# Two of a group's four value products issued one and two steps behind the turning of the maxima, instead of in front of it and in the next group

## The chip, the cores and the metric

One core of a Trainium2 chip runs the kernel. The metric is device time in microseconds (us). The kernel before took 1863.36 us (median of 3 runs, 1863.1 to 1865.16). A profiled execution of it took 1858.42 us.

## The reference

Four sequences of 512 tokens with 256 features go through four blocks: a cross-attention with 16 heads of 64, a gated fusion, a causal attention with 16 heads of 16, and a decoder layer with a banded self-attention (window 64), a full cross-attention (both 16 heads of 16) and a feed-forward part. The change touches the three attentions with heads of 16 only. Each computes, per head:

```python
s = jnp.einsum('bhqd,bhkd->bhqk', q, k) / jnp.sqrt(DH)
s = s + bias[None]                       # banded only
s = jnp.where(mask, s, -1e9)             # causal and banded
a = jax.nn.softmax(s, axis=-1)
o = jnp.einsum('bhqk,bhkd->bhqd', a, v)
```

## The kernel before, in words

The four sequences (B = 4) run one after the other in a hardware loop. In each, the three attentions with small heads follow each other: a = CAUSAL, BANDED, FULL. An attention's 16 heads are worked in GROUPS = 4 groups g of four heads, and the 512 rows in NT = 4 tiles of 128.

A group needs the scores twice. **Step A**(g, qt, u) (`pass_a`, L1220) is a pair of TensorE products, two heads u, queries in rows. VectorE takes their row maxima (`maxima`, L906). When the eight A of a group are through, **step M** (`maxima_cols`) splits the maxima into two bf16 halves. **Step T** (`turn_maxima`, L1267) turns them on TensorE, and ScalarE copies the turned rows into the query tile (`maxima_rows`, L675, two copies a group), so that the second pass of scores comes out with the maximum subtracted. **Step B**(g, kt, u) (`pass_b`, L1237) is that second pass with keys in rows; ScalarE exponentiates it (`exponentials`, L683). **Step V**(g, kt) (`values`, L1256) multiplies four heads' exponentials of key tile kt with the values and adds into a bank of `obank`; it waits for the exponentials of both B of its tile. **Step H**(g) (`head_out`) divides by the row sums on VectorE once V(g, 3) is done. Causal and banded products get masks added by further small products (L1206). Widths: 512 for every FULL product; 512, 384, 256, 128 for the causal B and V of kt 0 to 3 (A the other way round); 192 or 128 for banded ones. After the last group `out_heads` (L1296) projects; in the banded attention one projection stands before it.

A, B and T write to `ring`, which has SLOTS = 3 places. Each takes the place of the A, B or T three before it in the order of `group_steps`, and waits (`start`) until that one has been evacuated: A by VectorE, B and T by ScalarE. V writes to `obank` and takes no place in the ring. TensorE works in the order of `group_steps`; VectorE takes A, M and H from the same list, ScalarE B and T. Nothing overtakes on an engine. Groups overlap: while group g does its B and V, the A of group g+1 (second half) and of g+2 (first half) run between them.

The order of a middle group before, written as "B20" for B(g, 2, 0), A by its number 0 to 7 in its group, and V by kt:

```
i=0  B00  A4(g+1)  V2(g-1)
i=1  B01  A5(g+1)  V3(g-1)
i=2  B10  A6(g+1)
i=3  B11  A7(g+1)  M(g+1)  H(g-1)
i=4  B20  V0  T(g+1)  A0(g+2)  V1
i=5  B21  A1(g+2)
i=6  B30  A2(g+2)
i=7  B31  A3(g+2)
```

In group 2 the second half has no A, in group 3 there is none at all and no T; group 3 ends with V2, V3, H.

Of the kernel before, what the change touches and what calls it, by code (L numbers as in the profile page):

```python
# [29 lines left out]
NT = S // P  # L30
DT = D // P
H = 16
# [51 lines left out]
def ahead(g, n):  # L84

    return [("A", g) + divmod(n, 2)] if g < GROUPS else []


def group_steps(g):

    steps = []
    if g == 0:
        steps += ahead(1, 0) + ahead(1, 1) + [("T", 0)] + ahead(1, 2) + ahead(1, 3)
    for i in range(2 * NT):
        steps.append(("B", g) + divmod(i, 2))
        if i < NT:
            steps += ahead(g + 1, NT + i)
            if i < 2 and g:
                steps.append(("V", g - 1, 2 + i))
            if i == NT - 1:  # L100
                steps += [("M", g + 1)] if g + 1 < GROUPS else []
                steps += [("H", g - 1)] if g else []
            continue
        if i == NT:
            steps.append(("V", g, 0))
            steps += [("T", g + 1)] if g + 1 < GROUPS else []
        steps += ahead(g + 2, i - NT)
        if i == NT:
            steps.append(("V", g, 1))
    if g == GROUPS - 1:  # L110
        steps += [("V", g, 2), ("V", g, 3), ("H", g)]
    return steps


def attention_jobs(a):
    jobs = [(a, "A", 0, qt, u) for qt in range(NT) for u in range(2)]
    for g in range(GROUPS):
        jobs += [(a,) + step for step in group_steps(g) if step[0] in "ABT"]
    return jobs
# [33 lines left out]
def build(nc, io, out):  # L153
    with ExitStack() as ctx:
# [407 lines left out]
        def _(act):  # L562
# [20 lines left out]
            with act.Fori(0, B) as b:  # L583
# [102 lines left out]
                def attention(a):  # L686
                    for g in range(GROUPS):
                        for kind, *which in group_steps(g):
                            if kind == "T":
                                maxima_rows(a, *which)  # L690
                            if kind == "B":
                                if which == [0, NT - 1, 0]:
                                    for k in range(1, GROUPS):
                                        act.wait_ge(k_stacked[k], (b * 3 + a + 1) * 96)
                                exponentials(a, *which)
# [26 lines left out]
        def _(dve):  # L722
# [10 lines left out]
            with dve.Fori(0, B) as b:  # L733
# [201 lines left out]
                def attention(a):  # L935
                    for qt in range(NT):
                        for u in range(2):
                            maxima(a, 0, qt, u)
                    maxima_cols(a, 0)
                    for g in range(GROUPS):  # L940
                        for kind, *which in group_steps(g):
                            if kind == "A":
                                maxima(a, *which)
                            if kind == "M":
                                maxima_cols(a, *which)
                            if kind == "H":
                                head_out(a, *which)
# [501 lines left out]
```

How the kernel before makes its waits and increments, by code:

```python
        @block.sync  # L361
# [30 lines left out]
            def stack(a, b):  # L392
                k_high, k_low, q_high, q_low = ((0, 0), (3, 0)), ((1, 1),), ((0, 0), (1, 0)), ((3, 1),)
                sp.wait_ge(*drained_by(K_JOB[a], b))
                if a == CAUSAL:
                    sp.wait_ge(tiles_reset, b * TILES_RESET + TILES_RESET)
                else:
                    sp.wait_ge(*filled_by((a - 1, "B", GROUPS - 1, NT - 1, 1), b))
                    sp.wait_ge(q_preset, b * 2 * GROUPS + a * GROUPS)
                if a != BANDED:
                    sp.wait_ge(k_split, b * 3 + a + 1)
                    for g in range(GROUPS):
                        stack_k(a, b, g, k_high + k_low)
                    sp.wait_ge(q_hi_ready, (b * 3 + a + 1) * DT)
                    stack_q(a, b, 0, q_high)
                else:
                    stack_k(a, b, 0, k_high)
                    sp.wait_ge(q_hi_ready, (b * 3 + a + 1) * DT)
                    stack_q(a, b, 0, q_high)
                    sp.wait_ge(k_split, b * 3 + a + 1)
                    stack_k(a, b, 0, k_low)
                sp.wait_ge(*drained_by(Q_JOB[a], b))
                stack_q(a, b, 0, q_low)
                for g in range(1, GROUPS):
                    if a == BANDED:
                        stack_k(a, b, g, k_high + k_low)
                    stack_q(a, b, g, q_high + q_low)
# [16 lines left out]
                for t in range(NT):
                    sp.wait_ge(*filled_by(("V0", t), b))
                if b:
```

## Time and profile before

| | |
|---|---|
| median of 3 runs | 1863.36 us (1863.1 to 1865.16) |
| profiled execution | 1858.42 us, span 1856.3 us |
| granted TensorE clock, mean over the span | 0.948 of 2.4 GHz |
| busy: TensorE products, VectorE, ScalarE, GpSimd | 87%, 51%, 40%, 14% of the span |

A timeline row gives the start and the length in us, the engine (PE is TensorE, DVE VectorE, ACT ScalarE), the line, the operation, what it writes and reads, how many were merged, and in brackets how long the engine had been idle and who ended that. Products overlap, so the length of one is longer than the time until the next starts. The busy share is a mean over stages with different limits.

### The profile page before, as it was taken

Reading aid. Unit: us, or ns where it says so; the run is one execution under the profiler, and the core shown is the slowest. Engines: PE = TensorE matmul, PEld = TensorE weight load, DVE = VectorE, ACT = ScalarE, POOL = GpSimd, SP = SyncE. Lnnn points to the kernel's source line nnn. Section 1 sums busy time; section 2 is a strip of 40 time slices with the busy share of each in tenths; the row PEclk is TensorE's granted clock in tenths of the full one; section 3 lists DMA queues with packets and bytes.
Section 4 is the critical chain, followed back from the end, with each engine's and each line's share of the span. In section 5 each row is a group of like instructions: output and inputs, shape, how many; then the busy total and the mean of one; then the engine's idle time right before and its main releaser. Section 6 shows DMA issues by size and latency. Waiting matters only on the chain.

```text
span 1856.3 us, 27261 instructions
## 1 busy us (share of the span) xinstructions
PE 1623.5 (87%) x9592; PEld 816.9 (44%) x9592; DVE 949.5 (51%) x2240; ACT 737.9 (40%) x1281; POOL 254.0 (14%) x116
## 2 busy tenths in 40 slices
PE   5999898788999988888999898887899989888786
PEld 2226545434423655532532455553353255455234
DVE  2662655482465365547165447445616535645651
ACT  1652343254263233417236225252624621614352
POOL 1012111201101302110110221111011031112102
PEclk9999999899999899989999889898999998999899
DMA  8001103402100110340210021133111003022300
GB/s 320 1 6 35 35 2 69 94 10 108 47 1 6 35 35 15 56 102 1 108 47 1 7 44 25 33 70 70 42 69 45 1 8 60 9 52 51 59 23 12
DMA packets 44868, 84.17 MB, mean 45 GB/s; under 512 B 10416, under 2 KB 28592, under 8 KB 44464
## 3 DMA queue, kind: packets, MB, share of 16 engines
q1 hardware_dynamic: 44288, 78.42, 17.9%
q10 hardware_dynamic: 432, 3.83, 0.5%
q8 instruction: 86, 1.41, 0.3%
q14 instruction: 62, 0.51, 0.1%
HBM read 42.37 MB, written 2.10 MB: 24 GB/s over the span
## 4 chain that ended last, share of the span: by engine, by line
issue 35%; PE 33%; DVE 17%; ACT 7%; POOL 4%; SPq 3%; DMA 1%; DVEq 0%; ACTq 0%; POOLq 0%
PE ring L1045 6%; PE ring L1024 5%; DVE nmax L906 4%; DVE region_d L790 3%; PE obank L1017 3%; PE ring L1296 2%; PE obank L1256 2%; ACT region_e L607 2%; PE ring L1220 2%; SPq L382 2%; PE ring L1036 2%; ACT region_e L683 2%; PE ring L1237 2%; POOL q_all L530 2%; PE ring L1055 1%
## 5 line engine op out<-in xcount | busy, mean ns | idle before, releaser
L906 DVE TENSOR_REDUCE nmax<-ring 128x2 f32<-128x1024 f32 (+4 forms) x384 | 318.6, 854 | 179.4 <-PE ring L1206 116.7
L683 ACT ACTIVATE region_e<-ring 128x1024 f32<-128x1024 f32 (+4 forms) x384 | 268.9, 733 | 117.7 <-PE ring L1206 73.3
L790 DVE CUSTOM_DVE_ANT_0 region_d<-ring,maskb 128x512 f32<-128x512 f32 x256 | 165.8, 686 | 118.0 <-issue 117.8
L607 ACT ACTIVATE region_e<-region_d,nmin 128x512 f32<-128x512 f32 x256 | 182.6, 714 | 92.1 <-DVE nmin L790 86.1
L675 ACT ACTIVATE q_all<-ring 2x1024 fp32r<-2x1024 bf16 x96 | 97.6, 1016 | 256.1 <-PE ring L1267 255.6
L1017 PE MATMUL obank<-cbf 128*128 128x512 bf16 x672 | 174.1, 402 | 0.0
L1206 PE MATMUL ring<-cbf 64*128 64x128 bf16 (+1 forms) x2048 | 159.2, 240 | 0.0
L1083 PE MATMUL obank<-region_e,vs 128*64 128x512 f32 x512 | 139.9, 630 | 15.1 <-DVE vs L776 15.1
L1073 PE MATMUL ring<-region_q 64*128 64x512 f32 x512 | 141.3, 636 | 5.4 <-ACT region_q L596 5.4
L1220 PE MATMUL ring<-k_tiles_a,q_all 64*128 64x512 f32 (+4 forms) x384 | 84.2, 447 | 62.9 <-DMA q_all<-q_parts 51.7
L541 POOL TENSOR_TENSOR nat_x<-nat_n,rows 128x1024 f32<-128x1024 f32 x16 | 39.1, 2446 | 605.9 <-DVE nat_n L871 605.9
L1220 PE MATMUL ring<-k_tiles_b,q_all 64*128 64x512 f32 (+4 forms) x384 | 79.5, 410 | 23.3 <-ACT q_all L675 12.7
L1017 PEld LDWEIGHTS obank<-cbf 128*128 128x128 bf16 x672 | 63.4, 101 | 81.0 <-issue 24.1
L1237 PE MATMUL ring<-q_all,k_tiles_a 64*128 64x512 f32 (+4 forms) x384 | 79.7, 410 | 14.2 <-DVE nmax L906 11.8
L1237 PE MATMUL ring<-q_all,k_tiles_b 64*128 64x512 f32 (+4 forms) x384 | 74.6, 408 | 13.2 <-ACT q_all L675 8.5
L1220 PEld LDWEIGHTS ring<-k_tiles_a,q_all 64*128 64x128 f32 x384 | 41.1, 210 | 102.1 <-DMA q_all<-q_parts 48.5
L1296 PE MATMUL ring<-w_out,region_d 128*128 128x256 f32 x384 | 85.7, 381 | 0.0
L1073 PEld LDWEIGHTS ring<-region_q 64*128 64x128 f32 x512 | 39.7, 185 | 103.7 <-issue 93.2
L978 DVE TENSOR_TENSOR nat_y<-ring,nat_x 128x512 f32<-128x512 f32 x16 | 11.1, 692 | 138.9 <-PE ring L1045 123.3
L1256 PE MATMUL obank<-region_e,region_b 128*32 128x192 f32 (+4 forms) x1024 | 80.4, 390 | 1.4 <-ACT region_e L683 0.8
L515 POOL TENSOR_TENSOR q_all<-zero 128x2048 fp32r<-128x2048 f32 x8 | 28.8, 3623 | 382.9 <-PE ring L1073 382.9
L1055 PE MATMUL ring<-wvo,ctx_t 128*128 128x512 f32 x128 | 58.1, 609 | 25.3 <-ACT kcol L578 19.2
(169 smaller groups left out, 2291.4 us busy)
## 6 DMA issues: line engine op xcount, KB each, us to landing
q_all<-q_parts SPq DMA_DIRECT2D x288, 64.0 KB, 2.3
k_tiles_a<-k_parts SPq DMA_DIRECT2D x144, 64.0 KB, 2.3
k_tiles_b<-k_parts SPq DMA_DIRECT2D x144, 64.0 KB, 2.3
region_b<-in_w_f SPq DMA_DIRECT2D x8, 1024.0 KB, 5.1
wvo<-in_wv SPq DMA_DIRECT2D x4, 1024.0 KB, 8.9
wqk<-in_wq SPq DMA_DIRECT2D x4, 1024.0 KB, 11.1
wqk<-in_wk SPq DMA_DIRECT2D x4, 1024.0 KB, 13.1
wvo<-in_wo SPq DMA_DIRECT2D x4, 1024.0 KB, 5.6
```

What stands on the lines that cost most here:

```text
L607: ins = act.activation(e0[:, n % E0, h, :], sm0[:, n % 2, h, :], ACT.Exp, bias=nmin0[:, n, h:h + 1], scale=-1.0, accum_out=sum0[:, n, h:h ...
L683: act.activation(e16[:, n % 4, 2 * u:2 * u + 2, 0:nq], slot((a, "B", g, kt, u))[:, :, 0:nq], ACT.Exp)\
L790: ins = dve.tensor_tensor_reduce(out=sm0[:, n % 2, h, :], in0=slot(("S0", p, kt))[:, h, :], in1=maskb[:, :], scale=-1.0, scalar=3.0e38, op ...
L906: dve.tensor_reduce(nmax[:, qt, 2 * u:2 * u + 2], slot(name)[:, :, 0:nk], AX.X, ALU.max, negate=True)\
L1017: pe.matmul(obank[:, 0, :], cb("ident", P), cb("keyrows", S), start=True, stop=True)
L1073: ins = pe.matmul(dst[:, h, :], qk0[own, p % 2, 1, kt * P:(kt + 1) * P], qk0[own, p % 2, 0, :], start=True, stop=True)
L1083: ins = pe.matmul(obank[DK0 * h:DK0 * (h + 1), p % 2, :], vs0[:, n % 4, h, :], e0[:, n % E0, h, :], start=(kt == 0), stop=(kt == NT - 1))
L1206: ins = pe.matmul(dst[:, i, lo:lo + n], cb("halves", P, own, at=half * P), cb(table, n, own, at=half * whole + at), start=False, stop=(hal ...
L1220: ins = pe.matmul(dst[:, i, 0:nk], q_tiles[g][own, u, qt * P:(qt + 1) * P], k_tiles[g][own, u, k0:k0 + nk], start=True, stop=(a == FULL))
L1237: ins = pe.matmul(dst[:, i, 0:nq], k_tiles[g][own, u, kt * P:(kt + 1) * P], q_tiles[g][own, u, q0:q0 + nq], start=True, stop=(a == FULL))
L1256: ins = pe.matmul(obank[32 * s:32 * s + 32, (PAIRS + o) % 2, q0:q0 + nq], v_of[a][:, kt, h, :], e16[:, n % 4, s, 0:nq], start=(kt == 0), s ...
L1296: ins = pe.matmul(dst[j][:, i, 0:D], oT[:, t, m * P:(m + 1) * P], w_out[a][:, t, :], start=(t == 0), stop=(t == GROUPS - 1))
```

## The change

The second value product of a group is issued one step behind the T step (behind A1 of the group after next), and the third one step later (behind A2) instead of at the next group's first step. The fourth stays where it was. In the last group V1 and V2 follow B21 and B30, and only V3 is left behind B31. No instruction is added or dropped.

```diff
@@ group_steps
         if i < NT:
             steps += ahead(g + 1, NT + i)
-            if i < 2 and g:
-                steps.append(("V", g - 1, 2 + i))
+            if i == 1 and g:
+                steps.append(("V", g - 1, NT - 1))
@@
             steps.append(("V", g, 0))
             steps += [("T", g + 1)] if g + 1 < GROUPS else []
         steps += ahead(g + 2, i - NT)
-        if i == NT:
-            steps.append(("V", g, 1))
+        if NT < i < 2 * NT - 1:
+            steps.append(("V", g, i - NT))
     if g == GROUPS - 1:
-        steps += [("V", g, 2), ("V", g, 3), ("H", g)]
+        steps += [("V", g, NT - 1), ("H", g)]
```

The order of a middle group after:

```
i=0  B00  A4(g+1)
i=1  B01  A5(g+1)  V3(g-1)
i=2  B10  A6(g+1)
i=3  B11  A7(g+1)  M(g+1)  H(g-1)
i=4  B20  V0  T(g+1)  A0(g+2)
i=5  B21  A1(g+2)  V1
i=6  B30  A2(g+2)  V2
i=7  B31  A3(g+2)
```

## Rows read from the trace of the kernel before

**Rows 1.** Windows view, first sequence: causal, banded, full attention; busy us by engine, PEclk
```profile
core 0: us, PE busy (x) PEld busy (x) DVE busy (x) ACT busy (x) POOL busy (x), PEclk, DMA share, GB/s
206.59:256.59 50.00, 44.89 (x560) 23.88 (x559) 34.60 (x58) 29.82 (x40) 6.76 (x4) 1.00 0.09 16
288.86:334.35 45.49, 39.36 (x559) 25.97 (x559) 25.40 (x55) 22.23 (x40) 6.69 (x4) 0.93 0.30 53
364.33:431.77 67.44, 56.57 (x319) 18.72 (x319) 46.62 (x55) 39.50 (x40) 0.00 (x0) 0.91 0.13 26
```
**Rows 2.** Lines view by form: maxima, exponentials at full width, copies of the turned maxima
```profile
L906 DVE TENSOR_REDUCE nmax<-ring 128x2 f32<-128x1024 f32 x160 | 189.2, 1220 | 65.1 <-PE ring L1220 61.4 <-PE ring L1206 3.5
...
L683 ACT ACTIVATE region_e<-ring 128x1024 f32<-128x1024 f32 x160 | 157.8, 1028 | 53.0 <-PE ring L1237 36.9 <-PE ring L1206 14.3
...
L675 ACT ACTIVATE q_all<-ring 2x1024 fp32r<-2x1024 bf16 x96 | 97.6, 1016 | 256.1 <-PE ring L1267 255.6
```
**Rows 3.** Timeline, causal attention, from one T step to the next
```profile
222.83 0.62 PE L1267 MATMUL ring<-cbf,mcol 128*128 128x128 bf16 x8
...
223.49 2.04 ACT L675 ACTIVATE q_all<-ring 2x1024 fp32r<-2x1024 bf16 x2 [1.15 <-PE ring L1267]
...
223.76 0.85 PE L1256 MATMUL obank<-region_e,region_b 128*32 128x384 f32 x8
...
225.58 0.33 PE L1220 MATMUL ring<-k_tiles_b,q_all 64*128 64x128 f32 x2 [0.53 <-ACT q_all L675]
...
227.51 0.50 PE L1237 MATMUL ring<-q_all,k_tiles_a 64*128 64x512 f32 x2
...
228.25 1.02 ACT L683 ACTIVATE region_e<-ring 128x1024 f32<-128x1024 f32 x1 [0.81 <-PE ring L1206]
...
234.33 0.62 PE L1267 MATMUL ring<-cbf,mcol 128*128 128x128 bf16 x8
```
**Rows 4.** Timeline, causal attention: the last T step, and the last two value products
```profile
245.96 0.62 PE L1267 MATMUL ring<-cbf,mcol 128*128 128x128 bf16 x8
...
255.62 0.98 PE L1256 MATMUL obank<-region_e,region_b 128*32 128x256 f32 x16 [0.20 <-ACT region_e L683]
```
**Rows 5.** Timeline, banded attention: a T step, its V1, the next T, the projection behind
```profile
305.49 0.62 PE L1267 MATMUL ring<-cbf,mcol 128*128 128x128 bf16 x8 [0.40 <-DVE mcol L915]
...
306.43 0.53 PE L1256 MATMUL obank<-region_e,region_b 128*32 128x192 f32 x8
...
315.45 0.62 PE L1267 MATMUL ring<-cbf,mcol 128*128 128x128 bf16 x8 [0.40 <-DVE mcol L915]
...
334.28 1.98 PE L1024 MATMUL ring<-ctx_t,w_ck 128*128 128x512 f32 x4
```
**Rows 6.** Timeline, full attention of the second sequence: T, A0, V1, A1; two more T
```profile
844.45 0.62 PE L1267 MATMUL ring<-cbf,mcol 128*128 128x128 bf16 x8
...
845.00 0.50 PE L1220 MATMUL ring<-k_tiles_b,q_all 64*128 64x512 f32 x2
...
845.43 1.06 PE L1256 MATMUL obank<-region_e,region_c 128*32 128x512 f32 x8
...
847.21 0.50 PE L1220 MATMUL ring<-k_tiles_b,q_all 64*128 64x512 f32 x2 [0.28 <-ACT q_all L675]
...
847.75 4.67 DVE L906 TENSOR_REDUCE nmax<-ring 128x2 f32<-128x1024 f32 x4 [0.91 <-PE ring L1220]
...
857.76 0.62 PE L1267 MATMUL ring<-cbf,mcol 128*128 128x128 bf16 x8 [0.47 <-DVE mcol L915]
...
871.46 0.62 PE L1267 MATMUL ring<-cbf,mcol 128*128 128x128 bf16 x8 [0.47 <-DVE mcol L915]
```
**Rows 7.** Timeline, full attention of the second sequence: the last exponentials and the last V
```profile
882.29 2.85 ACT L683 ACTIVATE region_e<-ring 128x1024 f32<-128x1024 f32 x3 [0.67 <-PE ring L1237]
...
885.20 1.06 PE L1256 MATMUL obank<-region_e,region_c 128*32 128x512 f32 x8 [0.77 <-ACT region_e L683]
```
**Rows 8.** Windows view, full attention of the first sequence: before and after a clock step
```profile
390.60:394.00 3.40, 2.41 (x14) 0.89 (x10) 3.32 (x3) 2.77 (x4) 0.00 (x0) 1.00 0.02 5
394.00:397.40 3.40, 3.40 (x18) 0.90 (x20) 1.61 (x3) 1.43 (x2) 0.00 (x0) 0.50 0.00 0
```

## The prediction

> **What bounds the kernel now.** I read the windows view first, one window for each of the three attentions that the change touches. In the causal one TensorE is busy 44.89 of 50.00 us, against 34.60 for VectorE and 29.82 for ScalarE; in the full one 56.57 of 67.44, against 46.62 and 39.50 [rows 1]. No engine is full, so what counts is the order on TensorE and whom it waits for. I then walked the timeline from one T step to the next, because that distance is the price of a group, and looked at each bracket on a TensorE row.
>
> The same wait returns in every group. T is followed by ScalarE's two copies of the turned maxima, of 1.02 us each [rows 2]. They end about 2.7 us after T started (223.49 + 2.04 against 222.83) [rows 3]. A1 takes T's ring place, so A1 cannot start before that: 2.75 us behind T in the causal attention, 2.76 in the full one [rows 3, 6]. All that TensorE can do meanwhile is A0, V1 and B21. Even with V1 it still idles 0.53 us (causal) and 0.28 us (full) ahead of A1 [rows 3, 6]. **V1 costs nothing today**: it lies under a copy that A1 waits for anyway.
>
> **The change, part by part.** Instructions, widths and DMAs are the same; only V1 and V2 move. GpSimd's and SyncE's queues have nothing moved past them. H keeps its place behind V3, which keeps its place too.
>
> *V1 leaves the cover.* Between T and A1 only A0 and B21 are left, and A1 still starts at 2.75. V1 then stands behind A1 and delays B30, A2 and all that follows. Its length is about 0.8 us in the causal attention, 0.5 in the banded one and 1.0 in the full one (rows of 0.85, 0.53 and 1.06, less 0.06 in which the next product overlaps) [rows 3, 5, 6].
>
> *V2 leaves the next group's first step.* It goes behind A2, still on TensorE and still ahead of the same T, so it saves no time on a busy TensorE. It saves only where VectorE or ScalarE waited for what stood behind it. V2 never waits for ScalarE in its new place in groups 0 and 1: A2 in front of it takes B21's ring place and so has waited for the same exponentials.
>
> *Walk of a full-attention group,* times from T. From rows: T holds TensorE 0.55 (844.45 to 845.00), a pair ahead of a V 0.43, V 1.0, a pair ahead of another pair 0.34 (my estimate, from the 0.50 row less its overlap), maxima follow a product by 0.54 and take 1.17 to 1.22 [rows 2, 6], exponentials follow by about 0.6 and take 1.0 [rows 2, 3]. By these the order before comes to 13.35 from T to T where VectorE has no H, and 13.75 with it; the trace has 13.31 and 13.70 [rows 6]. That is the test of the rules. The order after: A0 0.55, B21 0.9, A1 2.75, V1 3.2 to 4.2, B30 4.2, A2 4.5, V2 4.95 to 5.95, B31 5.95, A3 6.3, B00 6.5, A4 7.6 (waits for the exponentials of B31, 6.55 to 7.55), B01 8.1, A5 8.6, V3 9.05 to 10.05, B10, A6 10.4, B11 10.6, A7 11.7 (waits for the exponentials of B10), its maxima 12.25 to 13.45, and T 0.55 later at 14.0. H (2.5 us on VectorE) has ended by A1's maxima and does not matter. So +0.65 and +0.25, **+0.9 us** for the two group passages with A.
>
> *The same for the causal group.* Here TensorE is nearly full, so V1's 0.8 is paid whole. One wait goes (0.24, B00 for A2's maxima), 0.2 comes from later waits and changes of kind of product. A new one comes: A5 takes B00's place, whose exponentials end 1.76 us after B00 started (227.51 to 228.25, and 1.02) [rows 3]. Before, V2 stood in between and covered it; now A5 waits 0.44. The sum is 12.7 from T to T against 11.50 [rows 3], +1.2. With H on VectorE I get +1.1. **+2.3 us.**
>
> *Banded.* By the same walk T to T becomes about 10.16. Before it was 9.96 [rows 5], and about 9.73 for the passage with H (my reading of the same view): **+0.6 us.**
>
> *The last group.* Before, V2 and V3 both stand behind B31; V2 runs while ScalarE exponentiates B31. After, V2 stands ahead of B31 and waits for the exponentials of B21, so B31 is issued late and V3 waits for it with nothing to cover. In the causal attention the end moves from 10.64 after T (256.60 − 245.96 [rows 4]) to 11.9: **+1.3**. In the full one ScalarE idles 0.67 once before [rows 7]; after, it idles so twice, ahead of B31 of group 2 and of group 3, and the end moves from 14.8 (885.20 + 1.06 − 871.46 [rows 6, 7]) to 15.6: **+0.8**. Banded: V3 waits about 0.5 for its exponentials, **+0.6**. The projections stand behind these ends on TensorE and move with them; H of group 3 stays hidden behind the first products of the projection.
>
> Sum for one sequence: causal 2.3 + 1.3, banded 0.6 + 0.6, full 0.9 + 0.8, together 6.5 us; times four, **+26 us**. From both sides: if only the bare covers count and later waits absorb the rest, it is V1's length in the causal passages (1.6), 0.4 in the banded ones, and V3's wait at the three ends (0.6 each), about 4 us a sequence, +16; if the walk misses waits as large as its own rounding (0.3 us for each of nine passages and ends, half of them hit), +32.
>
> *The clock.* In the full attention of the first sequence TensorE ran 14 products in 390.6 to 394.0, none of them a V, and then got 0.50 of 2.4 GHz for 3.4 us [rows 8]: up to 1.7 us of work lost, about 1.5 taken, since some of it would have been waiting. I count eight such falls inside the group loops (five full, three banded, none causal, whose granted clock is 1.00 [rows 1]). The change fills that stretch with V1 and V2, but it makes another: from V0's end to V1, some 3.5 us with T and three pairs, and 1.3 us of pure idle in it. I take the eight as moved and two or three as new in the causal attention, +4; bounds −12 (all eight gone, none new) and +12 (one in each of the eight causal passages).
>
> The profiled execution (1858.4, its span 1856.3) becomes 1888. It lies 5 us under the median of the runs; the difference carries over, so the median goes from 1863.4 to **1893**.
>
> **The rivals.** *1. The gaps absorb it: faster.* TensorE waits between A1 and V2's old place; V1 and V2 could fall into these gaps, the next group's start would lose V2's 1.0 us, and the clock would hold. Price: 1.0 for each of eight full passages and the eight falls, −8 −12: 1843. It decides where A1 need not wait for the copy. Against it: the copies have nearly one length (97.6 us for 96) [rows 2], and the causal attention has hardly a gap to fill.
>
> *2. The clock holds: slower by less.* TensorE now has V1 and V2 in the stretch that had none before the falls [rows 8], and the eight falls go without a new one: +26 − 12, 1877. For it: that is the stretch that the change fills. Against: the new stretch behind T is emptier still.
>
> The Trainium skill speaks for rival 2. "TensorE: Matmul & The Clock Gate", section "A second HAM failure mode: psum-queue depth-cycling", tells of a kernel that cycles through PSUM places, idles briefly between its groups of products, and whose clock swings between the two levels for that. By that rule filling the short gaps gives clock back. The falls behind stretches without a V agree with it; where the new gap behind T stands, no run here shows it yet.
>
> *3. New clock falls everywhere.* The stretch behind T drops the clock in each of the eight causal passages and in the five banded ones that had none: 13 × 1.5 = +20 on +26, 1910. For it: three pairs and T in 3.5 us, with masks the only other work. Against: V0 and V1 frame it closely.
>
> *4. Only the covers count.* The knock-on waits (A5, the late B31) are smaller than walked: +10 to +16, 1876.
>
> *5. Nothing moves.* The extra TensorE time is caught by waits for VectorE in each group: 1863. Against: A7's maxima and T hang directly on the delayed chain.
>
> **How the numbers follow.** Forecast 0.47, rival 1 0.06, rival 2 0.10, rival 3 0.15, rival 4 0.16, rival 5 0.06. The range takes in rivals 2 and 4, down to +16 − 6 (1873: the bare covers with four falls gone), and rival 3 (1911). Faster by over 0.2%, about what a measurement of this kernel can tell from none: rival 1, 0.06. Within: rival 5, 0.06. Slower: 0.88.
>
> **What would show it.** Right: A1 still 2.75 behind T with about 1.3 us idle ahead of it where 0.53 and 0.28 stood; T to T at 12.7 (causal) and 14.0 (full) where the clock holds; V3 of the last group alone behind B31, waiting. Wrong: T to T unchanged or shorter, A1 earlier, or a granted clock that holds through the full attention.

## The result, and the profile after

The change made the kernel **slower: 1916.48 us** (median of 6 runs, 1912.08 to 1921.76) against 1863.76 for the kernel before beside it, a ratio of 1.0282 [1.0258, 1.0307], or +52.7 us. Forecast were 1893 and at most 1911: the direction was right, the size was not.

The profiled execution took 1916.1 us. Its page, the span, the engines and the granted clock:

```profile
span 1914.0 us, 27261 instructions
...
PE 1656.7 (87%) x9592; PEld 836.5 (44%) x9592; DVE 951.6 (50%) x2240; ACT 738.9 (39%) x1281; POOL 253.9 (13%) x116
...
PEclk9998897889998989789999888878999988889899
```

The span grew by 57.7 us and TensorE's share stayed at 87%, so TensorE was busy longer over the same products: the mean granted clock fell from 0.948 to 0.927 (0.924 to 0.929 over the six runs). The windows view of the three attentions, first sequence, shows where (columns as in [rows 1]):

```profile
206.59:264.80 58.21, 49.66 (x570) 26.40 (x569) 35.58 (x61) 29.58 (x40) 7.81 (x5) 0.94 0.09 17
291.00:349.40 58.40, 46.99 (x565) 30.74 (x563) 26.03 (x59) 22.87 (x40) 7.43 (x5) 0.80 0.28 49
378.00:448.60 70.60, 57.35 (x319) 18.98 (x320) 46.88 (x56) 39.50 (x40) 0.00 (x0) 0.89 0.11 20
```

The causal attention had clock 1.00 and has 0.94; the banded one fell from 0.93 to 0.80, while its VectorE and ScalarE hardly work longer. The causal timeline, from T to T and then the last T and the last two V, answers [rows 3, 4]:

```profile
225.10 0.62 PE L1267 MATMUL ring<-cbf,mcol 128*128 128x128 bf16 x8
...
225.76 2.04 ACT L675 ACTIVATE q_all<-ring 2x1024 fp32r<-2x1024 bf16 x2 [1.15 <-PE ring L1267]
...
227.85 0.33 PE L1220 MATMUL ring<-k_tiles_b,q_all 64*128 64x128 f32 x2 [1.45 <-ACT q_all L675]
...
228.24 0.85 PE L1256 MATMUL obank<-region_e,region_b 128*32 128x384 f32 x8
...
229.80 1.08 PE L1256 MATMUL obank<-region_e,region_b 128*32 128x256 f32 x8
...
238.93 0.62 PE L1267 MATMUL ring<-cbf,mcol 128*128 128x128 bf16 x8 [0.20 <-DVE mcol L915]
...
252.86 0.62 PE L1267 MATMUL ring<-cbf,mcol 128*128 128x128 bf16 x8 [0.20 <-DVE mcol L915]
...
262.83 0.64 PE L1256 MATMUL obank<-region_e,region_b 128*32 128x256 f32 x8
...
264.34 0.42 PE L1256 MATMUL obank<-region_e,region_b 128*32 128x128 f32 x8 [0.48 <-ACT region_e L683]
```

A1 still starts 2.75 behind T, now with 1.45 us of idle time ahead of it where 0.53 stood, and V1 stands behind it. V2 (229.80), narrower than V1, takes 1.08 where V1 took 0.85, and the same width takes 0.64 in the last group, at full clock (262.83). So the clock has gone. Windows before and in that fall, then before and in one of the banded attention:

```profile
225.00:229.60 4.60, 3.05 (x46) 1.98 (x46) 0.89 (x3) 2.63 (x3) 0.00 (x0) 0.99 0.02 4
229.60:233.00 3.40, 3.40 (x34) 1.87 (x29) 1.38 (x2) 0.79 (x3) 1.39 (x1) 0.50 0.00 0
325.00:328.50 3.50, 1.95 (x34) 1.43 (x34) 2.91 (x8) 2.52 (x3) 0.00 (x0) 1.00 0.00 0
328.50:335.30 6.80, 6.80 (x74) 4.54 (x66) 2.53 (x5) 1.75 (x4) 1.89 (x1) 0.50 0.01 4
```

The stretch behind T has TensorE busy 3.05 of 4.60 us (causal) and 1.95 of 3.50 (banded); then it gets 0.50, the 1.2 GHz level, for 3.4 and 6.8 us, in which it never idles.

In the full attention, second sequence, T, A1 and T answer [rows 6]; ScalarE ahead of B31 of the last two groups, and the last V, answer [rows 7]:

```profile
886.86 0.62 PE L1267 MATMUL ring<-cbf,mcol 128*128 128x128 bf16 x8 [0.49 <-DVE mcol L915]
...
889.62 0.50 PE L1220 MATMUL ring<-k_tiles_b,q_all 64*128 64x512 f32 x2 [1.48 <-ACT q_all L675]
...
900.68 0.62 PE L1267 MATMUL ring<-cbf,mcol 128*128 128x128 bf16 x8 [0.48 <-DVE mcol L915]
...
906.02 7.44 ACT L683 ACTIVATE region_e<-ring 128x1024 f32<-128x1024 f32 x8 [0.67 <-PE ring L1237]
...
914.13 1.02 ACT L683 ACTIVATE region_e<-ring 128x1024 f32<-128x1024 f32 x1 [0.67 <-PE ring L1237]
...
915.21 1.06 PE L1256 MATMUL obank<-region_e,region_c 128*32 128x512 f32 x8 [1.12 <-ACT region_e L683]
```

T to T is 13.82 where the clock holds (900.68 − 886.86), ScalarE idles 0.67 twice instead of once, and the last V ends 15.59 behind T (916.27 − 900.68). The passage before this one has a fall; its T, A1 and V1:

```profile
871.54 0.62 PE L1267 MATMUL ring<-cbf,mcol 128*128 128x128 bf16 x8 [0.16 <-DVE mcol L915]
...
874.29 0.50 PE L1220 MATMUL ring<-k_tiles_b,q_all 64*128 64x512 f32 x2 [1.48 <-ACT q_all L675]
874.72 1.94 PE L1256 MATMUL obank<-region_e,region_c 128*32 128x512 f32 x8
```

V1 takes 1.94 where it took 1.06 [rows 6]: this fall begins right behind the wait ahead of A1. **The falls have moved.** Before, by the granted clock, those of a passage begin 5.2 to 6.9 us behind its T, like that of [rows 8]; after, every one of a passage, in all three attentions, begins 2.7 to 4.5 us behind its T. None is left where they were.

**The account.** I cut each of the twelve attentions (three in four sequences) from the first V to the end of the last V, before and after, and call that stretch its loop. Windows of before: a causal, a banded and a full loop without a fall, and the sum of all twelve:

```profile
221.63:256.59 34.96, 31.62 (x415) 16.18 (x411) 22.54 (x41) 24.22 (x34) 6.76 (x4) 1.00 0.01 2
304.56:334.35 29.79, 25.39 (x413) 16.34 (x411) 17.13 (x38) 18.24 (x34) 6.69 (x4) 1.00 0.15 28
...
843.24:886.27 43.03, 34.91 (x241) 11.23 (x239) 28.09 (x38) 33.49 (x35) 0.00 (x0) 1.00 0.06 17
...
sum 442.80, PE 378.86 PEld 178.68 DVE 271.14 ACT 304.00 POOL 53.84; mean PE 31.57 PEld 14.89 DVE 22.60 ACT 25.33 POOL 4.49
```

Windows of after: the first causal, banded and full loop, the fourth banded one, and the sum of all twelve:

```profile
223.90:264.76 40.86, 34.06 (x415) 17.48 (x411) 22.67 (x41) 23.99 (x34) 6.49 (x4) 0.92 0.01 2
311.28:349.31 38.03, 32.10 (x413) 20.79 (x411) 17.11 (x38) 18.87 (x34) 6.49 (x4) 0.78 0.12 22
401.93:448.51 46.58, 36.64 (x241) 11.48 (x239) 28.20 (x38) 33.48 (x34) 0.00 (x0) 0.95 0.02 4
...
1728.86:1760.01 31.15, 25.15 (x413) 16.24 (x411) 17.12 (x38) 18.55 (x34) 6.49 (x4) 1.00 0.12 22
...
sum 494.79, PE 404.87 PEld 194.79 DVE 272.29 ACT 304.98 POOL 52.15; mean PE 33.74 PEld 16.23 DVE 22.69 ACT 25.41 POOL 4.35
```

The loops grew from 442.80 to 494.79: 52.0 of the 57.7 us lie in them. The fourth banded loop has the same work as the first and the full clock; it is 6.9 us shorter. VectorE and ScalarE work 272.3 and 305.0 us in these windows, against 271.1 and 304.0.

### The profile page after: what moved, and what is told of

Its sections match the earlier page's. It is cut to its first block, busy times and chain, and to the rows that moved or that the text cites. A ratio compares the mean times of both kernels' runs of the same rounds, so it can differ in the third digit from the quotient of the medians.

```text
span 1914.0 us, 27261 instructions
## 1 busy us (share of the span) xinstructions
PE 1656.7 (87%) x9592; PEld 836.5 (44%) x9592; DVE 951.6 (50%) x2240; ACT 738.9 (39%) x1281; POOL 253.9 (13%) x116
## 4 chain that ended last, share of the span: by engine, by line
issue 35%; PE 34%; DVE 15%; ACT 8%; POOL 4%; SPq 3%; DMA 1%; DVEq 0%; ACTq 0%; POOLq 0%
PE ring L1045 6%; PE ring L1024 4%; PE obank L1256 3%; ACT region_e L683 3%; DVE nmax L906 3%; DVE region_d L790 3%; PE ring L1220 3%; PE obank L1017 3%; PE ring L1296 2%; ACT region_e L607 2%; SPq L382 2%; PE ring L1036 2%; PE ring L1237 2%; POOL q_all L530 2%; PE ring L1055 1%
## 5 line engine op out<-in xcount | busy, mean ns | idle before, releaser
L1206 PE MATMUL ring<-cbf 64*128 64x128 bf16 (+1 forms) x2048 | 177.7, 260 | 0.0
L1220 PE MATMUL ring<-k_tiles_b,q_all 64*128 64x512 f32 (+4 forms) x384 | 85.4, 441 | 48.5 <-ACT q_all L675 33.8
L1256 PE MATMUL obank<-region_e,region_b 128*32 128x192 f32 (+4 forms) x1024 | 90.6, 430 | 13.7 <-ACT region_e L683 13.7
L1237 PE MATMUL ring<-q_all,k_tiles_a 64*128 64x512 f32 (+4 forms) x384 | 85.7, 441 | 6.0 <-DVE nmax L906 3.8
L1256 PE MATMUL obank<-region_e,region_c 128*32 128x512 f32 x512 | 73.2, 646 | 13.7 <-ACT region_e L683 13.7
L1237 PE MATMUL ring<-q_all,k_tiles_b 64*128 64x512 f32 (+4 forms) x384 | 79.2, 424 | 2.3 <-ACT region_e L683 1.4
L925 DVE STREAM_TRANSPOSE rbuf<-obank 128x512 f32<-128x512 f32 x48 | 34.3, 714 | 92.2 <-issue 92.2
```

The lines of the kernel that those rows point to most:

```text
L1206: ins = pe.matmul(dst[:, i, lo:lo + n], cb("halves", P, own, at=half * P), cb(table, n, own, at=half * whole + at), start=False, stop=(hal ...
L1220: ins = pe.matmul(dst[:, i, 0:nk], q_tiles[g][own, u, qt * P:(qt + 1) * P], k_tiles[g][own, u, k0:k0 + nk], start=True, stop=(a == FULL))
L1237: ins = pe.matmul(dst[:, i, 0:nq], k_tiles[g][own, u, kt * P:(kt + 1) * P], q_tiles[g][own, u, q0:q0 + nq], start=True, stop=(a == FULL))
L1256: ins = pe.matmul(obank[32 * s:32 * s + 32, (PAIRS + o) % 2, q0:q0 + nq], v_of[a][:, kt, h, :], e16[:, n % 4, s, 0:nq], start=(kt == 0), s ...
```

## The experiments

The table gives all kernels first; each ratio is against the kernel before on the same chip. "Half clock" is the time at 0.50 of 2.4 GHz in the four loops of an attention by the granted clock of the profiled execution. T to T and end (last T to end of last V) are of passages without such time; where all had some, that is said. The windows and the half clock are of one execution of each kernel, the medians of several.

| kernel | median us | ratio to before | half clock: causal, banded, full | T to T and end, causal | T to T and end, full |
|---|---|---|---|---|---|
| before | 1863.8 | 1 | 0, 10.2, 17.1 | 11.50, 11.63, 10.63 | 13.30, 13.70, 14.81 |
| after | 1916.48 | 1.0282 [1.0258, 1.0307] | 34.1, 52.2, 15.4 | 13.83, 13.93 (both with 3.4), 11.90 | 15.33 (with 3.4), 13.82, 15.59 |
| e1_v1_covered | 1874.69 | 1.0050 [1.0023, 1.0077] | 0, 27.3, 8.7 | 11.61, 11.75, 12.25 | 13.20, 13.48, 16.36 |
| e2_v2_back | 1885.23 | 1.0113 [1.0086, 1.0141] | 27.3, 20.5, 14.7 | 12.28 (second, once), 10.71 | 13.89 (second), 14.03 |
| e3_gap_filled | 1876.88 | 1.0065 [1.0038, 1.0093] | 0, 11.2, 3.1 | 12.40, 12.40, 11.90 | 13.80, 13.80, 15.60 |
| e7_gap_two | 1872.60 | 1.0051 [1.0034, 1.0069] | 0, 6.8, 0 | 12.40, 12.40, 11.90 | 13.81, 13.80, 15.60 |
| e9_gap_one | 1888.11 | 1.0117 [1.0085, 1.0149] | 0, 34.1, 9.8 | 12.41, 12.41, 11.90 | 13.80, 13.81, 15.59 |
| e4_tail_before | 1909.98 | 1.0222 [1.0190, 1.0254] | 30.7, 68.3, 13.3 | as after, 10.63 | as after, 14.81 |
| e8_before_filled | 1854.02 | 0.9949 [0.9931, 0.9967] | 0, 6.8, 15.2 | as before | as before |
| e5_hybrid | 1849.42 | 0.9918 [0.9899, 0.9937] | 0, 13.7, 3.6 | as before | 13.20, 13.48, 14.03 |
| e6_hybrid_filled | 1839.87 | 0.9867 [0.9849, 0.9884] | 0, 13.7, 3.3 | as before | 13.20, 13.49, 14.03 |

### The two halves of the change apart

e1 leaves V1 behind A0 as before, and moves V2 alone:

```diff
         steps += ahead(g + 2, i - NT)
-        if NT < i < 2 * NT - 1:
-            steps.append(("V", g, i - NT))
+        if i in (NT, NT + 2):
+            steps.append(("V", g, 1 if i == NT else 2))
```

> The change with its first half undone: the second value product V1 stands behind A0 again, under the copy of the turned maxima; the third, V2, stays behind A2. Cover theory (V1 was free under the copy, its loss opens an idle gap that costs V1's length and brings the clock falls): A1 starts 2.75 us behind T with under 0.6 us of idle time ahead of it, the causal attention keeps a granted clock of 1.00, what is left is the late B31 of the last group (about 2.7 us a sequence), so 1862 to 1878 us. Rival (V2 on the chain between A2 and B31 is what costs): stays above 1890 us.

e2 takes the kernel before and moves V1 alone:

```diff
         steps += ahead(g + 2, i - NT)
-        if i == NT:
+        if i == NT + 1:
             steps.append(("V", g, 1))
```

> The change with its second half undone: V1 behind A1 as in the change, V2 in the next group's first step and, in the last group, behind B31 as in the kernel before. Cover theory: V1's exposed length costs 2 to 3 us a sequence, the end of the last group costs nothing, and the clock falls come in as many passages as with the change or more, so 1888 to 1912 us. Rival (V2 is what costs): back at 1863 to 1872 us.

Measured: +11.5 us for V2 alone, +22.0 for V1 alone (1885.23, just under its range); together they cost 52.7, so 19 come only with both. The timeline of e1, T and A1 of the first causal passage:

```profile
224.36 0.62 PE L1267 MATMUL ring<-cbf,mcol 128*128 128x128 bf16 x8
...
227.12 0.33 PE L1220 MATMUL ring<-k_tiles_b,q_all 64*128 64x128 f32 x2 [0.53 <-ACT q_all L675]
```

and its first causal loop in the windows view:

```profile
223.16:259.97 36.81, 31.52 (x415) 16.04 (x411) 22.65 (x41) 23.88 (x34) 6.50 (x4) 1.00 0.01 2
```

The same of e2:

```profile
222.87 0.62 PE L1267 MATMUL ring<-cbf,mcol 128*128 128x128 bf16 x8
...
225.62 0.33 PE L1220 MATMUL ring<-k_tiles_b,q_all 64*128 64x128 f32 x2 [1.45 <-ACT q_all L675]
```

```profile
221.66:260.68 39.02, 34.14 (x415) 17.60 (x411) 22.60 (x41) 24.30 (x34) 6.71 (x4) 0.91 0.01 1
```

A1 stands 2.76 and 2.75 behind T in both, so V1 never delayed it. With V1 in front the idle time is 0.53 and the causal clock is whole; with V1 behind it is 1.45 and the clock falls in the causal loops of all four sequences (27.3 us at half clock), though V2 stands where it stood. V1's leaving its cover makes the falls there. V2's move is no loss in itself: in the full attention e1's passages are shorter than before's (13.20 and 13.48 against 13.30 and 13.70), and no fall begins in them, where five did before; in the causal one they are 0.1 longer. It loses at the ends, 12.25 against 10.63 and 16.36 against 14.81, and all four banded ends carry a fall, where one did before.

### Filling the gap ahead of A1

If the idle time makes the falls, useless products in it must bring the clock back at no cost to the order. e3, e7 and e9 are the changed kernel with five, two and one products of a zero block ahead of A1, added into the group's open sum, which stays the same (the zero block is set once at the start). The edit of e3; e7 has 2 and e9 has 1 where it says 5:

```diff
                         for kind, *which in group_steps(g):
...
+                            if kind == "A" and which[1:] == [0, 1] and g + 2 == which[0]:
+                                for _ in range(5):
+                                    pe.matmul(obank[:, (PAIRS + a * GROUPS + g) % 2, :], zeros_bf[:, :],
+                                              cb("keyrows", S), start=False, stop=False, skip_group_check=True)
```

> The change, with five extra products of 512 columns issued between B21 and A1, in the gap where TensorE waits for the copy. They add zeros to the group's bank, so the result is that of the change, and end before A1 can start. Clock theory (of the 53 us, 26 are order and the rest clock falls that the idle gap brings): falls inside the causal group loops gone, granted clock there 1.00, T to T 12.7 us in the causal attention, 1872 to 1892 us. Rival (order alone costs over 45 us, the clock little): stays above 1905 us.

> The change with two, not five, extra products of 512 columns in the gap ahead of A1; they add zeros. They end inside the gap, so the order of everything else stays. Clock theory: the time lies between that with none (1916 us) and that with five (1877 us), with fewer falls in the causal passages than the change has; 1880 to 1905 us. If the gain with five came from anything but the filled gap, no such step shows.

> The change with a single extra product of 512 columns in the gap ahead of A1, adding zeros. With two the time was 1873 us, with none 1916. If the clock follows the filling by degrees, 1885 to 1905 us; if one product is already enough to hold it, 1870 to 1880 us; if it needs two, above 1905 us.

Measured, by the ratios: of the 53 us that the change cost, 12 are left with five products (1.0065), 9.5 with two (1.0051) and 22 with one (1.0117). The mean granted clock of every run of e7 lies at 0.954 to 0.961, against 0.924 to 0.929 of after. e7 came out below its bracket of 1880 to 1905: two did as much as five. e7's timeline from T to T in the first causal passage (its lines stand two lower, L1269 is T), with one of the two zero products (the record of the other is missing):

```profile
223.48 0.62 PE L1269 MATMUL ring<-cbf,mcol 128*128 128x128 bf16 x8
...
224.95 0.38 PE L1289 MATMUL obank<-cbf,zeros_bf 128*128 128x512 bf16 x1 [0.16 <-issue]
...
226.24 0.33 PE L1222 MATMUL ring<-k_tiles_b,q_all 64*128 64x128 f32 x2 [0.91 <-ACT q_all L677]
...
231.02 0.44 PE L1222 MATMUL ring<-k_tiles_b,q_all 64*128 64x384 f32 x2 [0.20 <-ACT region_e L685]
...
235.88 0.62 PE L1269 MATMUL ring<-cbf,mcol 128*128 128x128 bf16 x8 [0.19 <-DVE mcol L917]
```

A1 is 2.76 behind T as ever, and T to T is 12.40 where after had 13.83. Windows of e7: the first causal and full loop, the second banded one, and the sum of the twelve:

```profile
222.28:260.18 37.90, 32.19 (x417) 16.29 (x415) 22.64 (x41) 24.00 (x34) 6.49 (x4) 1.00 0.01 2
...
390.62:435.05 44.43, 35.29 (x244) 11.43 (x243) 28.31 (x38) 33.49 (x35) 0.00 (x0) 1.00 0.02 5
...
764.59:795.74 31.15, 25.92 (x415) 16.50 (x415) 17.12 (x38) 18.55 (x34) 6.50 (x4) 1.00 0.15 26
...
sum 456.85, PE 376.64 PEld 178.30 DVE 272.32 ACT 304.62 POOL 51.93; mean PE 31.39 PEld 14.86 DVE 22.69 ACT 25.38 POOL 4.33
```

These are the order's own prices, free of the clock: T to T is the same with one, two and five products, so the products add nothing to it, and after's one banded loop without a fall takes the same 31.15. Against before's loops without a fall (34.96, 29.79 and 43.03) the order costs 2.94 (causal), 1.36 (banded) and 1.37 to 1.40 (full) a sequence, 5.7 together and **22.7 us in four**. What the loops lost beyond that, 52.0 − 22.7 = **29.3 us, is the clock**: they stood at half clock for 27.3 us before and for 101.7 after. This is a remainder; the price of a fall checks it. A fall of 3.4 us costs 1.43 in the causal passage (13.83 − 12.40), 1.5 in the full one (15.33 − 13.81); 6.8 us cost 2.69 in a banded passage (12.92 − 10.23) and 2.40 in a causal one (14.80 − 12.40). At these 0.35 to 0.44 us for each us of half clock, the 74.4 us more make 26 to 33.

With one product the causal loops hold their clock; three of the four banded loops and three of the four full ones don't. The median of 1888 lies in the range that I had given for filling that works by degrees. e9's first causal and second banded loop:

```profile
223.68:261.58 37.90, 31.39 (x415) 16.21 (x413) 22.64 (x41) 24.03 (x34) 6.49 (x4) 1.00 0.01 2
...
775.23:812.05 36.82, 30.81 (x413) 19.72 (x413) 17.13 (x38) 18.88 (x34) 6.49 (x4) 0.81 0.08 15
```

### The ends

e4 is the changed kernel with groups 2 and 3 in the order before: V1 at its old place there, V2 of group 2 in group 3's first step, V2 and V3 of group 3 behind B31.

```diff
 def group_steps(g):
+    if g >= GROUPS - 2:
+        steps = group_steps_before(g)
+        if g == GROUPS - 2:
+            steps.remove(("V", g - 1, 2))
+        return steps
...
```

> The change in groups 0 and 1 only; groups 2 and 3 issue their steps as in the kernel before. By the walk the late B31 and the uncovered V3 cost 1.3 (causal), 0.6 (banded) and 0.8 us (full) a sequence, so this is 10 to 11 us under the change, and a little more if clock falls in those groups go too: 1897 to 1908 us. If the end of an attention is hidden behind what follows, it equals the change, 1912 to 1920 us.

Measured: 1909.98, a little above the range. The three ends are back at 10.63, 9.16 and 14.81 to a hundredth where no fall lies in them, against 11.90, 9.75 and 15.59 after, so they had cost 1.27, 0.59 and 0.78, or 2.6 us a sequence and 10.6 in all. The loops fell by 7.2 only (494.79 to 487.56), for the banded ones stand at half clock for 68.3 us against 52.2: all eight of their passages fall, where six did, and two ends fall for 6.8 us each (11.55), where two of after did for 3.4 and 11.2. Whether the edit does that, or one execution differs from the next, is not shown. The medians moved by 6.5 us, the ratios by 11, and their intervals, 5 to 6 us to either side, don't tell these apart.

### The kernel before, filled; and a mixed order

e8 is the kernel before with the same zero products ahead of A1, none in the causal attention, three in the banded and one in the full one:

```diff
+                            if kind == "A" and which[1:] == [0, 1] and g + 2 == which[0]:
+                                for _ in range({CAUSAL: 0, BANDED: 3, FULL: 1}[a]):
+                                    pe.matmul(obank[:, (PAIRS + a * GROUPS + g) % 2, :], zeros_bf[:, :], ...
```

> The kernel before, its order untouched, with three extra products (banded) and one (full attention) that add zeros in the gap ahead of A1. If the eight falls of its group loops come from that gap, some of their 12 us return: 1851 to 1860 us. If they come from the stretch behind A1, in which no V ran, filling the gap ahead of A1 does not help: 1861 to 1867 us. I lean to the second for the full attention, whose gap is 0.28 us.

Measured: 1854.02, 0.9949. The time lies in the range for falls that come from the gap; the loops don't bear that out. Windows of its first full and its second banded loop:

```profile
385.81:430.30 44.49, 36.33 (x241) 11.75 (x241) 28.14 (x38) 33.50 (x35) 0.00 (x0) 0.96 0.05 16
...
759.18:789.14 29.96, 26.58 (x417) 16.76 (x417) 17.13 (x38) 18.25 (x34) 6.70 (x4) 1.00 0.15 27
```

In the full attention half clock stays at 15.2 us (17.1 before), and the falls that begin in its passages still do so 6.0 to 6.7 us behind T. So the full attention's falls do not come from the gap ahead of A1; that leaves the stretch without a V of [rows 8], and e5 below fills it. No banded passage falls, where two of eight fell before, and one end falls, for 6.8 us where one did for 3.4. That the gap made those two falls is not shown: two against none, in one execution each, is little, and they began 5.2 and 5.3 us behind T. All loops together gained only 1.7 us (441.06 against 442.80), of 4.4 between the profiled executions and 9.8 between the medians. Outside them the time at half clock went from 167.6 to 149.0 us; why filling the loops should do that is not settled.

e5 puts the parts together that gained: V2 behind A2 in groups 0 and 1 of the banded and full attentions, V1 behind B21 in groups 2 and 3 of the full one, the causal one untouched. e6 adds e8's products to it.

```diff
+def early_v2(a, g):
+    return a != CAUSAL and g < GROUPS - 2
...
-            if i < 2 and g:
+            if i < 2 and g and not (i == 0 and early_v2(a, g - 1)):
                 steps.append(("V", g - 1, 2 + i))
...
-        if i == NT:
+        if i == (NT + 1 if a == FULL and g >= GROUPS - 2 else NT):
             steps.append(("V", g, 1))
+        if i == NT + 2 and early_v2(a, g):
+            steps.append(("V", g, 2))
```

> The kernel before, with the pieces of the change that cost no cover: V1 stays under the copy of the turned maxima; V2 goes behind A2 in groups 0 and 1 of the banded and full attention only; in groups 2 and 3 of the full attention V1 goes behind B21. The causal attention and all other ends are as before. Cover theory: T to T 9.7 us (banded), 13.2 and 13.5 us (full), end of the full attention 14.0 us behind its last T, 6 us in all, and up to 10 us of clock falls gone: 1847 to 1860 us. Rival (any V taken out of its old place costs): above 1866 us.

> The kernel of the run before it in this list (V2 behind A2 in groups 0 and 1 of the banded and full attention, V1 behind B21 in the last two groups of the full one), with extra products that add zeros in what is left of the gap ahead of A1: three in the banded and one in the full attention. Clock theory: the remaining falls between T steps go; 1843 to 1857 us. If the gap there is too short to bring a fall, no difference to the kernel without them (within 4 us).

Measured: 1849.42 (0.9918) and 1839.87 (0.9867); **both are faster than the kernel before, by 0.8% and 1.3%, and than the changed one.** The third full loop of e5:

```profile
1296.02:1337.96 41.94, 35.22 (x241) 11.35 (x239) 28.13 (x38) 33.16 (x35) 0.00 (x0) 1.00 0.04 11
```

That is 1.1 less than before's best (43.03), with the full clock in two of four sequences and 3.6 us at half clock in all, where 17.1 stood; no fall begins in a passage of it. V2 behind A2 fills the stretch that had no V, as the prediction said of the change; kept apart from the gap behind T, it pays. e6 came out below its range of 1843 to 1857, but its loops gained nothing on those of e5 (433.0 against 432.4 us): what its products gave lies outside them, as most of e8's gain does, and why is not shown.

## Why the prediction was wrong

**What held.** *A1's wait:* 2.75 behind T, with 1.45 (causal), 1.48 (full) and 0.99 (banded) us idle in front. *V1 exposed:* shown by e2 and e1. *The order's price:* 22.7 us against a walk of 26.

| term, us | predicted | measured, clock held |
|---|---|---|
| causal T to T | 12.7 | 12.40 |
| banded T to T | 10.16 | 10.23 |
| full T to T | 14.0 | 13.81 |
| ends behind the last T, causal, full | 11.9, 15.6 | 11.90, 15.60 |
| banded end | +0.6 | +0.59 |
| order, four sequences | +26 | +22.7 |
| clock, in the loops | +4 | +29.3 |

The causal passage was over-walked at A5: the wait that I put at 0.44 is 0.20 in e7 (231.02 above). The ends came out to a tenth.

**The step that failed is the clock term.** I took the eight falls as moved and two or three as new, +4, bounded by +12. The price of a fall of 3.4 us was right (1.5 taken, 1.43 to 1.5 measured); the number and the length of the falls were wrong. In the full attention the eight did move, one kind for the other: the five falls behind the stretch without a V went, four behind the gap ahead of A1 came, one in the first passage of each sequence (15.4 us at half clock, 17.1 before), and with the gap filled (e7) there is none. In the causal one, which had none to give back, a fall came into every one of the eight passages, two of them of 6.8 us, and in the banded one six of eight passages and two ends fell, mostly for 6.8 us, one for 11.2. Net of the order, by loops: causal +13.6, banded +15.6, full +0.1. Of the banded 15.6, 4.6 lie at the ends (11.26 and 14.08 against 9.75 after, 10.44 against 9.16 before); there the gap is not shown to be the cause, since two of four banded ends fall in e4 and e5 too, whose ends are in the order before.

My working already had the reason: 1.3 us of pure idle behind T. But I weighed it against the stretch of [rows 8], which the change fills, as if one paid for the other everywhere. They act apart: e2 makes the gap and brings the causal falls, e8 fills it and leaves the full attention's. Only the full attention had enough of the old falls to pay for the new. The bound of +12 was too low as well: one fall of one length in eight causal passages, and none counted in the banded ones.

**The rivals.** Rival 3, new falls everywhere, was in the main what happened, at 0.15. Even its 1910 is short by 6, since it counted one fall of 3.4 us for a passage and none at the ends. What I set against it, that V0 and V1 frame the gap closely, was no row of the trace. Rival 2 was half right: the old falls went, but four came in the full attention, where the gain is 1.7 us of half clock, and more elsewhere. The rule of the Trainium skill that I set beside it ("TensorE: Matmul & The Clock Gate", section "A second HAM failure mode: psum-queue depth-cycling"), frequent short idle times between groups of products are enough to swing the clock, agrees with the runs, above all for the gap that the change makes: in the causal loops 0, 34.1 and again 0 us at half clock before, after and with two zero products (e7). It spoke for rival 3 as well, and I had read it for only one of the two stretches. Rivals 1, 4 and 5 fail by the order's 22.7 us alone.

**From profile to median.** I let the 5 us between the profiled execution of before and its median carry over. It did not: after's profile (1916.1) lies at its median. By profiled executions the forecast was short by 28 us (+30 against +57.7), by medians by 23.

**Open.** The medians grew by 52.7 us, the profiled executions by 57.7: that of before lies 5 us under its median, and all that is told by loops goes by one execution of each kernel. Of the 57.7 us, 5.7 lie outside the loops, where half clock went from 167.6 to 178.8 us; that it is the cause was not tried. Nor do the runs say which sequence falls: the fourth banded loop of after has the order of the other three, and no fall.

## What to carry to other kernels

Work that lay under a wait was free twice here: it took no time there, and it kept TensorE's clock up. Moving such work out is to be priced with a fall of the clock in every passage as the upper bound (here eight of eight causal, six of eight banded and four of eight full ones), and not with a few on average. Where a wait can't be filled with work, a cheap product of zeros into an open sum is worth a trial, and its effect is to be looked for in the granted clock of that stretch: in e8 against before, and in e6 against e5, the time fell mostly elsewhere. Try the parts of a reordering apart, and per stage: here V2's move was a gain in the passages of the full attention and a loss at every end.

## What the runs showed of the hardware

One zero product per passage, about 0.22 us, was enough to keep the clock in all eight causal passages of e9, though by e7's rows some 1.1 us of idle time was left ahead of A1 (0.91 behind the second product, and that product's 0.22). In the banded and full attentions of the same run it was not enough. The length is from e3's row of four:

```profile
225.55 1.03 PE L1289 MATMUL obank<-cbf,zeros_bf 128*128 128x512 bf16 x4 [0.16 <-issue]
```

One takes 0.38 by e7's row, so each further one adds (1.03 − 0.38) / 3 = 0.22. And a fall costs less than half of its time at half clock when TensorE is busy in it: 1.43 of 3.4 us, where 1.7 would be half. What hides the rest was not tried.
